# Attention row scaling moved from VectorE to ScalarE, and two ScalarE copies moved ahead of its exponential

## The reference

```python
x = x + conv(x)                       # 1x1 product, gelu, low-pass, 1x1 product
t = t + attn(_ln_t(t), ...)           # the block that the change touches
t = t + ffn(_ln_t(t), ...)            # 8 experts, top 2

def _ln_t(v, eps=1e-05):
    m = jnp.mean(v, axis=-1, keepdims=True)
    s = jnp.var(v, axis=-1, keepdims=True)
    return (v - m) / jnp.sqrt(s + eps)

q = (x @ Wq + bq).reshape(b, s, 12, 16)
k = (x @ Wk + bk)                     # one head of 16, shared by the 12 heads
v = (x @ Wv + bv)
attn = softmax(einsum(q, k))          # over j; k and v do not depend on j
```

## Time and profile before

| what | value |
|---|---|
| median of 3 runs | 528.34 us (527.46, 528.34, 532.61) |
| the profiled execution's own time | 531.54 us |
| its span in the trace | 529.7 us |
| busy share of the span | PE 77%, PEld 70%, DVE 60%, POOL 48%, ACT 36% |
| attention phase, first DVE instruction to last of ACT | 74.28 to 197.48 us |
| granted TensorE clock, mean of the execution | 0.854 |

### The profile page before, as it was taken

One profiled execution on the slowest core, in us unless ns is written; L12 is line 12 of the kernel. 1 busy time (PEld: TensorE's weight loads), 2 busy tenths in 40 slices (PEclk: granted clock), 3 DMA queues, 4 the chain that ended last, 5 costly groups with the idle time before them and its releaser, 6 DMA issues.

```text
span 529.7 us, 9212 instructions
## 1 busy us (share of the span) xinstructions
PE 405.9 (77%) x2236; PEld 369.0 (70%) x2237; DVE 316.7 (60%) x764; ACT 191.7 (36%) x417; POOL 255.5 (48%) x369
## 2 busy tenths in 40 slices
PE   5699928578877571474999999999999998998300
PEld 5699827466766470463999999999999997998200
DVE  1266672788866818992555555555556554655164
ACT  3443503413332110001555555555555554554200
POOL 0155542455555310464466666666666665664200
PEclk9999999777777555555999999999999998999855
DMA  7988510022222212001122222222222222222398
GB/s 206 243 198 226 134 57 0 22 64 62 62 62 71 72 40 45 1 0 37 44 72 70 71 69 71 72 67 69 69 71 70 68 72 62 62 71 61 97 345 302
DMA packets 47391, 47.07 MB, mean 89 GB/s; under 512 B 14313, under 2 KB 40332, under 8 KB 47372
## 3 DMA queue, kind: packets, MB, share of 16 engines
q1 hardware_dynamic: 40460, 30.04, 20.8%
q0 software_dynamic: 6912, 16.82, 10.9%
HBM read 32.16 MB, written 14.68 MB: 88 GB/s over the span
## 4 chain that ended last, share of the span: by engine, by line
PE 40%; DMA 5%; issue 3%; SPq 2%; POOL 2%; DVE 1%; ACT 1%; POOLq 0%; ACTq 0%; DVEq 0%
PE moe_ps_y L1148 7%; PE moe_ps_h L1134 4%; PE moe_ps_x L1114 3%; DMA moe_xt<-rows,moe_idx 3%; DMA wa_hi<-chosen_rows 2%; PE moe_ps_u L1123 2%; PE moe_ps_u L1124 2%; PE moe_ps_u L1126 2%; PE moe_ps_gt L1123 2%; PE moe_ps_u L1127 2%; PE moe_ps_u L1125 2%; PE moe_ps_y L1150 2%; PE moe_ps_gt L1124 2%; PE moe_ps_gt L1127 2%; PE moe_ps_gt L1125 2%
## 5 line engine op out<-in xcount | busy, mean ns | idle before, releaser
L1062 POOL DMA_INDIRECT moe_xt<-rows,moe_idx x72 | 72.9, 1012 | 61.8 <-POOL moe_idx L1059 22.3
L1071 POOL DMA_INDIRECT chosen_rows<-moe_y,moe_idx x72 | 71.1, 988 | 35.9 <-issue 20.6
L1148 PE MATMUL moe_ps_y<-wd,moe_h_hi 128*128 x216 | 72.4, 360 | 1.3 <-DVE moe_h_lo L1279 0.6
L1224 ACT ACTIVATE moe_yy<-moe_ps_y,moe_xt 128x384 f32<-128x384 f32 x72 | 41.9, 581 | 75.7 <-PE moe_ps_y L1148 71.9
L1287 DVE TENSOR_TENSOR moe_y<-moe_yy 128x192 f32<-128x192 f32 x72 | 26.1, 362 | 60.6 <-ACT moe_yy L1224 59.0
L1204 ACT ACTIVATE moe_x_hi<-moe_ps_x 128x256 fp32r<-128x256 f32 x72 | 27.7, 384 | 90.0 <-PE moe_ps_x L1115 88.2
L1263 DVE TENSOR_TENSOR moe_x_lo<-moe_ps_x,moe_x_hi 128x128 fp32r<-128x128 f32 x72 | 21.0, 292 | 44.9 <-issue 23.0
L1148 PEld LDWEIGHTS moe_ps_y<-wd,moe_h_hi 128*128 128x128 f32 x216 | 40.9, 190 | 4.8 <-issue 4.3
L1279 DVE TENSOR_TENSOR moe_h_lo<-moe_ps_h,moe_h_hi 128x384 fp32r<-128x384 f32 x72 | 40.2, 558 | 2.8 <-ACT moe_h_hi L1216 0.5
L1273 DVE TENSOR_TENSOR moe_hid<-moe_ps_u,moe_sg 128x384 f32<-128x384 f32 x72 | 39.5, 548 | 1.8 <-PE moe_ps_u L1127 1.8
L1150 PE MATMUL moe_ps_y<-wd,moe_h_lo 128*128 x144 | 36.1, 251 | 0.0
(11 more groups left out here) (185 smaller groups left out, 1173.2 us busy)
## 6 DMA issues: line engine op xcount, KB each, us to landing
wa_hi<-chosen_rows SPq DMA_DIRECT2D x16, 384.0 KB, 6.2
xs<-in_x SPq DMA_DIRECT2D x8, 384.0 KB, 6.0
conv_stage<-in_wgu SPq DMA_DIRECT2D x8, 384.0 KB, 3.7
conv_stage<-in_wgu SPq DMA_DIRECT2D x16, 192.0 KB, 4.6
rows<-attn_xr SPq DMA_DIRECT2D x8, 384.0 KB, 2.7
out<-xs SPq DMA_DIRECT2D x8, 384.0 KB, 6.2
attn_stage<-in_down SPq DMA_DIRECT2D x8, 288.0 KB, 3.3
conv_xta<-in_xT SPq DMA_DIRECT2D x8, 256.0 KB, 4.3
```

The costliest lines, as they stand in the source:

```text
L1062: nc.gpsimd.indirect_dma_start(xt[:, slot, :], None, rows.ap(), bass.IndirectOffsetOnAxis(ap=idx[:, slot, 0:1], axis=0)).then_inc(gathered ...
L1071: nc.gpsimd.indirect_dma_start(chosen_rows.ap(), bass.IndirectOffsetOnAxis(ap=idx[:, slot, 1:2], axis=0), y[:, slot % YR, :], None).then_i ...
L1148: ins = nc.tensor.matmul(both, hi, halves, start=(k == 0), stop=(k == 2))
L1224: nc.scalar.activation(yy[:, s].rearrange("p h c -> p (h c)"), ps_y[:, s, 0:2 * C], ACT.Copy, scale=xt[:, slot, bass.ds(GC + e, 1)]).then_ ...
```

## The change

1. The mean is no longer kept. POOL's `row_deviation` computes `minus = -mean` in place of a copy of the mean, then rstd as before, and then, by one instruction more, `shift = minus * rstd`. So a normalised row is `xs * rstd + shift`. This is in the convolution and in attention.
2. `norm`, the scaling of the rows for q, k and v, is four ACT instructions (Identity with a scale and a bias per row) in place of four of DVE. `norm_route` stays on DVE, with `xs * rstd + shift`, and waits for dev_done, the semaphore of shift.
3. On DVE norm stood up to two quads ahead: norm(n+2) in step n. On ACT it stands one ahead: norm(n+1) at the start of step n.
4. On ACT out_of_psum(n+1) moves from the start of step n to a place after split(n) and before exponential(n).

The rows of PE are unchanged, and so are those of POOL but for the instruction more in `row_deviation`. The diff, cut to its core:

```diff
-def row_deviation(nc, pool, q, s, mv, vtmp, half, mean, rstd, mv_done, eps_done, pow_done, mean_done, pool_turn):
+def row_deviation(nc, pool, q, s, mv, vtmp, minus, half, shift, rstd, mv_done, eps_done, pow_done, mean_done,
+                  dev_done, pool_turn):
...
-    nc.gpsimd.tensor_copy(mean[:, bass.ts(q, QT)], mv[:, s, :, 0]).then_inc(mean_done, 1)
+    nc.gpsimd.tensor_scalar(minus[:, s, :], mv[:, s, :, 0], -1.0, None, ALU.mult).then_inc(mean_done, 1)
     pool.wait_ge(eps_done, made(q))
     pool.sem_inc(pool_turn, 1)
     nc.gpsimd.tensor_tensor(rstd[:, bass.ts(q, QT)], vtmp[:, s, :], half[:, 0:1].broadcast_to([P, QT]),
                             ALU.pow).then_inc(pow_done, 1)
+    pool.wait_ge(pow_done, made(q))
+    pool.wait_ge(mean_done, made(q))
+    pool.sem_inc(pool_turn, 1)
+    nc.gpsimd.tensor_tensor(shift[:, bass.ts(q, QT)], minus[:, s, :], rstd[:, bass.ts(q, QT)],
+                            ALU.mult).then_inc(dev_done, 1)
...
-        ins = nc.vector.tensor_scalar(dst[:, t, :], xs[:, at, :], mean[:, bass.ds(at, 1)],
-                                      rstd[:, bass.ds(at, 1)], ALU.subtract, ALU.mult)
+        ins = nc.vector.tensor_scalar(dst[:, t, :], xs[:, at, :], rstd[:, bass.ds(at, 1)],
+                                      shift[:, bass.ds(at, 1)], ALU.mult, ALU.add)
...
             @block.scalar
+                def norm(i, s):
+                    q = quad(i, s)
+                    act.wait_ge(tr_done, freed(q))
+                    for t in range(QT):
+                        at = bass.ds(QT * q + t, 1)
+                        ins = nc.scalar.activation(xn[:, s, t, :], xs[:, at, :].rearrange("p t c -> p (t c)"),
+                                                   ACT.Identity, scale=rstd[:, at], bias=shift[:, at])
+                    ins.then_inc(xn_done, 1)
...
+                norm(0, 0)
                 out_of_psum(0, 0)
                 for n in range(LAG):
+                    norm(*turned(0, n + 1))
+                    copy_products(*turned(0, n), route=False)
+                    split(*turned(0, n))
                     out_of_psum(*turned(0, n + 1))
-                    copy_products(*turned(0, n), route=False)
-                    attend(*turned(0, n))
+                    exponential(*turned(0, n))
                 with act.Fori(LAG // RING, last) as i:
                     for r in range(1, 1 + RING):
-                        out_of_psum(*turned(i, r + 1))
+                        norm(*turned(i, r + 1))
                         route_out_of_psum(*turned(i, r - LAG))
                         copy_products(*turned(i, r))
-                        attend(*turned(i, r))
+                        split(*turned(i, r))
+                        out_of_psum(*turned(i, r + 1))
+                        exponential(*turned(i, r))
...
             @block.vector
-                norm(0, 0)
-                norm(0, 1)
                 for n in range(RING):
-                    norm(1, n)
                     scores(0, n)
...
                 with dve.Fori(1, last) as i:
                     for s in range(RING):
-                        norm(i + 1, s)
                         norm_route(i - 1, s)
                         scores(i, s)
```

More of the change, by code:

```diff
@@ L103, in program @@
         xs = keep("xs", [P, TILES, C])
-        mean, rstd = keep("mean", [P, TILES]), keep("rstd", [P, TILES])
+        shift, rstd = keep("shift", [P, TILES]), keep("rstd", [P, TILES])
         lg = keep("lg", [P, TILES, EXPERTS])
@@ L353, in deviation @@
                 def deviation(i, s):
-                    row_deviation(nc, pool, quad(i, s), s, mv, vtmp, half, mean, rstd, mv_done, eps_done,
-                                  pow_done, mean_done, pool_turn)
+                    row_deviation(nc, pool, quad(i, s), s, mv, vtmp, minus, half, shift, rstd, mv_done, eps_done,
+                                  pow_done, mean_done, dev_done, pool_turn)
                 split(0, 0)
@@ L482, in transposes, with attention_phase @@
     return ins
-def attention_phase(nc, xs, mean, rstd, eye, wqa, wqb, cos_t, sin_t, ga, gb, rows, row_tiles, down, wd, lg):
+def attention_phase(nc, xs, shift, rstd, eye, wqa, wqb, cos_t, sin_t, ga, gb, rows, row_tiles, down, wd, lg):
     with ExitStack() as stack:
@@ L614, in _ @@
             def _(act):
+                act.sem_inc(xn_done, RING)
                 act.sem_inc(ev_done, RING)
@@ L743, in _ @@
                 nc.vector.memset(xb[CB:CB + 1, :, :], 1.0).then_inc(bias_row, 1)
-                for c in (xn_done, xr_done, prod_done, score_done, diff_done, den_done, rec_done, wt_done, res_done,
+                for c in (xr_done, prod_done, score_done, diff_done, den_done, rec_done, wt_done, res_done,
                           stats_done, mv_done):
                     dve.sem_inc(c, RING)
-                def norm(i, s):
-                    q = quad(i, s)
-                    dve.wait_ge(tr_done, freed(q))
-                    normalise(nc, dve, q, xs, mean, rstd, xn[:, s]).then_inc(xn_done, 1)
                 def norm_route(i, s):
@@ L756, in norm_route @@
                     dve.wait_ge(rtr_done, freed(q))
-                    dve.wait_ge(pow_done, made(q))
-                    normalise(nc, dve, q, xs, mean, rstd, xr[:, s]).then_inc(xr_done, 1)
+                    dve.wait_ge(dev_done, made(q))
+                    normalise(nc, q, xs, shift, rstd, xr[:, s]).then_inc(xr_done, 1)
                 def scores(i, s):
```

22 lines of the change are left out of this document (12 added, 10 removed).

## The result

| | before | changed |
|---|---|---|
| median of the runs | 529.54 us (4 runs, 527.46 to 532.61) | 573.60 us (4 runs, 569.64 to 575.81) |
| the profiled execution | 531.54 us | 573.68 us |
| its span, mean granted clock | 529.7 us, 0.854 | 571.9 us, 0.825 |

The changed kernel takes 1.0787 times as long, 95% interval [1.0734, 1.0840]; the quotient of the two medians above is 1.083, inside it. The forecast was 571 us in a range of 560 to 584, and 573.60 lies in that range. By the medians the loss is 44 us, by the ratio 42.

What follows compares the result with a forecast made beforehand. Attention's step was taken to be set by a loop of waits, no engine full. The terms sum to +42.75 us on the profiled 531.54, giving 574.3, or 571 us for a median, range 560 to 584.

Steps and rivals of the forecast that it cites:

- start of the phase and norm(0): Attention's start: norm(0) no longer waits for DVE's memset, but the convolution's added POOL instruction delays the phase; together +0.1 us.
- steps 1 and 2: Attention steps without a router part: 15.9 us each from exponential to exponential, two 31.8 against 20.55, +11.25 us.
- steps 3 to 6: Attention steps with the router part: 19.85 us each, four 79.4 against 49.63, +29.8 us.
- step 7: Last exponential-to-exponential stretch, without a turn: projection(7) starts early and out_of_psum's move works, 11.4 against 11.76, -0.3 us.
- the router's rest: End of attention: norm_route(6) waits for shift instead of rstd, the added POOL instruction losing its cover, +0.3 us.
- The order on ACT: Attention loop: norm behind exponential(n-1) makes overlapping work run in sequence, PE idle about 9.6 us a step.
- Norm on ACT: Four ACT instructions in attention: 1.75 us with fixed addresses, 2.0 us in the loop.
- PE's block and route matmuls: PE in steps 3 to 6: turn, turn_route and projection 7.55 us, then route matmuls 2.6 us.
- the two clock rivals: TensorE's clock in attention: stays low, 591 us, chance 0.05; or stays high, 557 us, chance 0.04.
- table load: Rival on ACT: each norm and exponential brings a 1.28 us load, 14 in all, 589 us; chance 0.01.
- POOL's instruction beside PE's block: Attention loop: the added shift instruction on POOL runs beside PE's work and is covered except once, at the end.
- The other side: Rival: PE's work still runs beside kk and scores, attention loses copies and DVE's norm, 523 us; chance 0.03.

Runs made afterwards that it cites:

- e2: Kernel before, with norm(n+2) still on DVE but moved behind scores(n), no shift, nothing moved on ACT: 564.88 us, 1.0664.
- e4: Changed kernel with ACT's loop written out and norm one quad earlier, norm(n+2) between the router's copies and the copy of the projection: 533.39 us, 1.0061.
- e9: Changed kernel with only PE's row reordered, projection(n) ahead of turn(n+1) and turn_route(n-3): 554.26 us, 1.0488.
- e6: Changed kernel with out_of_psum(n+1) back at the start of the step, behind norm(n+1): 572.68 us, 1.0820.
- e10: Changed kernel with ACT's loop over the steps written out, in the same order, as a control: 569.23 us, 1.0771.
- e1: Kernel before with only the shift arithmetic and its added POOL instruction, norm staying on DVE at its old place: 533.51 us, 1.0079.
- e3: Kernel before with only out_of_psum(n+1) moved behind split(n), ahead of exponential(n), norm on DVE: 531.42 us, 1.0028.
- e7: Kernel before with route_out_of_psum(n-3) put ahead of out_of_psum(n+1) on ACT: 528.90 us, 0.9995.
- e8: e7 plus weights(n) ahead of residual(n-1) on DVE and weigh_value(n) ahead of deviation(n-1) on POOL, against the kernel before: 528.84 us, 0.9995.

## Why the prediction was right, point by point

The times are from the two profiled executions.

| step | forecast | measured |
|---|---|---|
| start of the phase and norm(0) | +0.1 | +1.6 |
| norm(1) | +1.6 | +1.7 |
| steps 1 and 2 | +11.25 | +10.4 |
| steps 3 to 6 | +29.8 | +28.4 |
| step 7 | -0.3 | +1.7 |
| the router's rest | +0.3 | +0.5 |
| routing and experts | 0 | -2.0 |
| sum | +42.75 | +42.2 |

*The order on ACT* was right and carries nearly all: the signs named ahead are there (xn behind each exponential, PE idle 9.05 to 9.72 us in each of six steps, DVE's wait for kk 9.26, ACT's wait for the difference 4.50). e2 and e4 show it by experiment: lateness on the old engine makes the loss, lead on the new one takes it back. e9 shows the second half of the argument, that the projection is held because it is queued behind the turn: 16 to 18 us come back by its place alone.

*Norm on ACT* was taken at 1.75 and 2.0 us and took 1.84 with fixed addresses and 1.86 in the loop. The estimate by the Trainium skill, page "ScalarE: Activation LUTs", section "What ACT_TABLE_LOAD costs", was 1.85 us, nearer than mine from the neighbouring row.

*PE's block and route matmuls* were taken together as 10.15 us; the four steps took 10.6, 9.05, 10.0 and 10.45. The clock came out between the two clock rivals, PEclk 0.67 in the mean: 1.2 GHz behind the idle time, and then 2.4 GHz, where a projection group takes 0.57 us. In three of the four steps the first groups still took 1.00 or 1.01; in step 4 all eight were fast. Both rivals fell in steps 3 to 6, and no table load is in ACT's timeline between exponential and norm. The term was right by the middle of two values, which is partly luck: the same pieces took 9.0 to 10.5 us in e6 and 9.0 to 10.1 in e10, 1.7 and 2.1 us less over the four steps. In e6's step 1 the low clock lasted through the whole block.

*Step 7 failed*, by 2.0 us. The prediction said that projection(7) starts right behind the previous route matmuls and is done by about exponential(6), and that out_of_psum's move works here. It did not start then:

```profile
199.56 0.27 PE L489 MATMUL attn_ps_rb<-eye,attn_xr 128*64 128x128 f32 x1
201.63 1.14 PE L600 MATMUL attn_ps_q<-wqa,attn_xa 128*128 128x240 f32 x2 [1.79 <-ACT attn_xb L646]
...
207.36 1.01 PE L601 MATMUL attn_ps_q<-wqb,attn_xb 65*128 65x240 f32 x2
208.16 0.43 PE L606 MATMUL attn_ps_q<-ga,attn_ra 128*128 128x8 f32 x2
...
211.67 0.59 PE L607 MATMUL attn_ps_q<-gb,attn_rb 64*128 64x8 f32 x2
```

The moved copies put xb(7) behind copy_products(6) and split(6); PE waited 1.79 us for it, and the granted clock of step 7 is 0.50, thus 1.2 GHz: the eight groups took 1.01 us each, the first 1.14, and the route matmuls 4.1 in place of 2.6. e6 takes this wait away. Its projection was done at 205.56, and the step was still 12.83 us, because then PE stood idle for the router's copies and the route matmuls ran at the low clock all the same:

```profile
204.99 0.57 PE L601 MATMUL attn_ps_q<-wqb,attn_xb 65*128 65x240 f32 x2
208.06 0.59 PE L606 MATMUL attn_ps_q<-ga,attn_ra 128*128 128x8 f32 x2 [2.50 <-ACT attn_rb L652]
```

So about 1.5 us of the miss are route matmuls at the low clock and 0.6, the difference between the changed kernel and e6, the wait for xb.

*The start of the phase* was undersized, by 1.5 us. DVE's first instruction of the phase, with the idle time before it, in the kernel before and then in the changed one:

```profile
74.28 0.91 DVE L743 MEMSET attn_xb<- 1x1024 f32 x1 [2.25 <-PEq L179]
```

```profile
75.76 0.91 DVE L765 MEMSET attn_xb<- 1x1024 f32 x1 [3.14 <-PEq L180]
```

The idle time at the barrier, with the added POOL instruction and its wait ahead of it, is 0.9 us longer, where I took 0.3. The rest is in the convolution: in five traces of kernels with the mean the phase starts at 72.57 to 74.28 us (mean 73.2), in eight with shift at 74.13 to 75.83 (mean 74.7). Why the convolution itself ends later was not tried.

*POOL's instruction beside PE's block* is hidden in the changed kernel, as said: in steps 3 to 6 POOL is through with it and waits another 6.1 to 7.7 us for ACT before rotate_key. This holds only while the loop is long: in the 12.4 us steps of e1 and e4 rotate_key follows POOL's row without a wait.

*Routing and experts* were 2.0 us shorter, all of it in the experts (281.6 against 283.6 us from their first transpose). None of the kernels changes the experts. The five traces with the mean have 282.8 to 284.7 us (mean 283.5), the eight with shift 280.5 (e10) to 283.7 (mean 282.1). The ranges overlap, so scatter is likely, but an effect of some 1.5 us is not excluded; it was not tried.

*The sum* came closer than its parts. The start and step 7 ran 3.5 us over the forecast, steps 1 to 6 2.25 us under it and the experts 2.0 under it, and that these cancel is luck. Also, the profiled execution of the kernel before is 2.0 us above the median of its four runs; by the medians the loss is 44 and not 42 us.

*The other side*, a faster kernel, rested on xn being early enough. e4 grants it that, and it still isn't faster. Its own sum seems wrong too: it left out the wait for xb (e3) and POOL's loop (e4).

No order tried beats the kernel before; e7 and e8 tie with it.

## What to carry to other kernels

Where engines work in order, ask of a moved step what stands ahead of it in its new row and what that waits for, then what is queued behind its consumer: an engine with room to spare (ACT, 32% busy in those steps) can still be the wrong place. One quad of lead was worth 37 us (e4 against e10), where the longer instruction was worth under 1 us a step (e2's 18.7 us against the changed kernel's 19.5, shift included). An operation hidden by a long loop can come back onto the path once the loop is mended. A step that only a few iterations have, the last one above all, needs its own timeline, with the clock that the idle time ahead of it leaves.

## What the runs showed of the hardware that was not expected

With the same order on PE and the same wait of 9.0 us for xn, step 1 had two slow projection groups in the changed kernel (1.00 and 0.81 us, then 0.57), four in e10 (1.00, then 0.66 and 0.57) and eight in e6 (1.01). The step took 14.9, 15.9 and 17.5 us. Differences of 1 or 2 us between single traces of such a loop say little.

Sixteen route matmuls of 8 columns took 2.6 us where PE had waited 1.25 us behind transposes at high clock (e9, step 4), 4.3 us where it had waited 1.16 us behind transposes at low clock (e9, step 3), and 4.2 us where it had waited 2.50 us behind a projection that had ended at the fast 0.57 us a group (e6, step 7).

The same POOL multiplication of weigh_value took 1.65 us in step 4 of e4, where DVE's norm_route ran beside it, and 2.23 us in step 4 of e8, where DVE's residual and statistics did. That DVE's work is the cause is a reading of the overlap, not tried alone.
